# Another hand-written order of work in the stretch between the first feed-forward block and attention

## The reference

```python
x = x + 0.5 * ffn(layernorm(x))      # 8 routed experts
x = x + attn(layernorm(x))           # the stage that matters here
x = x + 0.5 * ffn(layernorm(x))
```

```python
h = (x - mu) * rsqrt(var + eps) * ln_scale + ln_bias     # a second norm, inside attn
c_q, c_kv = h @ w_down_q.T, h @ w_down_kv.T               # latents, 64 wide each
q, k, v = up(c_q), up(c_kv), up(c_kv)                     # 16 heads of 64
q, k = rope(q), rope(k)                                   # rotation by position
out = softmax(q @ k.T / 8) @ v @ w_out.T + residual
```

## Time and profile before

| what | value |
|---|---|
| median of 3 runs | 1592.28 us (1590.46 to 1593.84) |
| profiled execution | 1590.73 us |
| its span on the core | 1588.9 us |
| PE busy | 1520.2 us, 96% |
| DVE busy | 1437.3 us, 90% |
| POOL busy | 1318.8 us, 83% |
| ACT busy | 1254.2 us, 79% |
| chain that ended last | PE 83%, DVE 6%, issue 4%, POOL 3%, ACT 2%, DMA 1% |

### The profile page before, as it was taken

How to read it: one execution, slowest core, us unless ns; L and a number is a source line. 1 busy time by engine, 2 the same in 40 slices (tenths; PEclk the granted TensorE clock), 3 DMA queues, 4 the chain that set the end, 5 groups by cost and what they waited for, 6 DMA issues and landing times.

```text
span 1588.9 us, 48489 instructions
## 1 busy us (share of the span) xinstructions
PE 1520.2 (96%) x19224; PEld 996.8 (63%) x19224; DVE 1437.3 (90%) x2912; ACT 1254.2 (79%) x1764; POOL 1318.8 (83%) x924
## 2 busy tenths in 40 slices
PE   4999869999999999999999999999999999987998
PEld 3777535666666666666666666666666666654555
DVE  6657789999999999999999999999999998967897
ACT  4443577888888888888888888888888888885654
POOL 2566548999999999999999999999999997764666
PEclk9999999999999999999999999999999999999999
DMA  7333130212111121212121211111221212003443
GB/s 203 115 116 118 34 80 12 57 46 53 41 43 42 42 51 43 51 32 52 32 52 45 58 42 42 42 42 46 48 52 32 52 32 52 21 2 101 129 135 120
DMA packets 65727, 95.68 MB, mean 60 GB/s; under 512 B 11744, under 2 KB 24544, under 8 KB 65248
## 3 DMA queue, kind: packets, MB, share of 16 engines
q1 hardware_dynamic: 62416, 91.66, 21.9%
q10 hardware_dynamic: 3088, 0.92, 0.3%
HBM read 39.72 MB, written 2.36 MB: 26 GB/s over the span
## 4 chain that ended last, share of the span: by engine, by line
PE 83%; DVE 6%; issue 4%; POOL 3%; ACT 2%; DMA 1%; ACTq 0%; POOLq 0%; DVEq 0%
PE ps L1020 14%; PE ps L994 14%; PE ps L1021 14%; PE ps L1040 8%; PE ps L1042 8%; PE ps L1038 8%; PE ps L523 3%; PE ps L1009 3%; PE ps L1002 2%; PE ps L501 2%; POOL area L681 2%; PE ps L503 2%; PE ps L502 2%; PE ps L988 2%; PE ps L987 2%
## 5 line engine op out<-in xcount | busy, mean ns | idle before, releaser
L1384 POOL TENSOR_TENSOR area<-area 128x1024 f16<-128x1024 f32 (+1 forms) x512 | 833.5, 1647 | 81.7 <-ACT area L1301 72.6
L1172 DVE TENSOR_REDUCE area<-ps 128x1 f32<-128x512 f32 x1024 | 664.9, 684 | 11.2 <-PE ps L994 8.7
L1299 ACT ACTIVATE area<-ps 128x1024 f16<-128x1024 f32 x512 | 525.5, 1026 | 142.5 <-PE ps L1021 142.3
L1040 PE MATMUL ps<-cv_all,area 128*128 128x64 f16 x4096 | 457.3, 195 | 0.0
L1038 PE MATMUL ps<-cv_all,area 128*128 128x65 f16 x4096 | 455.5, 193 | 0.6 <-POOL area L1384 0.5
L1042 PE MATMUL ps<-cv_all,area 128*128 128x65 f16 x4096 | 454.2, 192 | 0.0
L1040 PEld LDWEIGHTS ps<-cv_all,area 128*128 128x128 f16 x4096 | 381.9, 97 | 78.9 <-issue 0.3
L1038 PEld LDWEIGHTS ps<-cv_all,area 128*128 128x128 f16 x4096 | 384.5, 97 | 60.1 <-issue 9.0
L994 PE MATMUL ps<-area 128*128 128x512 f16 x1024 | 388.5, 380 | 4.8 <-DVE area L1172 4.8
L1020 PE MATMUL ps<-area 128*128 128x512 f16 x1024 | 389.2, 380 | 3.6 <-DVE cv_all L1213 1.1
L1021 PE MATMUL ps<-area 128*128 128x512 f16 x1024 | 389.3, 380 | 0.0
(11 more groups left out here) (173 smaller groups left out, 2265.5 us busy)
## 6 DMA issues: line engine op xcount, KB each, us to landing
area<-area SPq DMA_DIRECT2D x384, 128.0 KB, 2.7
area<-f_w_rows_in_dram SPq DMA_DIRECT2D x126, 256.0 KB, 3.3
xg<-in_x SPq DMA_DIRECT2D x4, 512.0 KB, 9.3
out_x<-xg SPq DMA_DIRECT2D x3, 512.0 KB, 5.0
area<-in_wup SPq DMA_DIRECT2D x1, 1024.0 KB, 9.1
cs<-in_rope SPq DMA_DIRECT2D x1, 1024.0 KB, 9.9
area<-area SPq DMA_DIRECT2D x64, 2.0 KB
area<-in_wg SPq DMA_DIRECT2D x1, 512.0 KB, 7.9
```

The costliest lines, as they stand in the source:

```text
L1040: nc.tensor.matmul(o[:, 0:DH], p_hi[:, s % 4, c:c + P], latents[:, DH + 1:CV], start=False, stop=False, skip_group_check=True)
L1172: nc.vector.tensor_reduce(mx[:, hd, kh, qt:qt + 1], bank, AX.X, ALU.max).then_inc(s_mr, 1)
L1299: nc.scalar.activation(p_hi[:, s % 4, :], sc, ACT.Exp, scale=0.125).then_inc(s_e16, 1)
L1384: nc.gpsimd.tensor_tensor(p_lo[:, s % 4, c0:], src[:, (s // 2) % 2, :], p_hi[:, s % 4, c0:], ALU.subtract).then_inc(s_pp, 1)
```

## The change

Only the four strings change, so the same instructions are issued with the same waits, in another order on each engine.

```diff
-        pe_start = "trrlrrrrtrtrltrrrlrtlataaablaaaaaaaabtalralababmbbbrbSbb"
-        dve_start = "lrrlrrrrrrlNrNrNrNlraaalabaaaaaaaablalraababmbbblrbbb"
-        act_start = "nfnnhfhncxfcfnchfxxcnhfnxhnxxhfxcxfhhc"
-        pool_start = "ssoossssooossooossssoooos"
+        pe_start = "trrtlrrrtrrlrrtlrrtrlaaaatalaaabbtabaaalbalabaabmrrSbbbb"
+        dve_start = "lrrlrrrrrlNrNrNNrlrraaalaaaaabbabalaalbaabaabmlrrbbbb"
+        act_start = "nfnnhfhncfxfnnhchxfccxnhfncfxhxcfxhxxh"
+        pool_start = "ssssoosoosssoooossoossoos"
```

## The result

| | before | changed |
|---|---|---|
| median | 1590.49 us (10 runs, 1587.15 to 1593.84) | 1585.03 us (10 runs, 1582.94 to 1587.35) |
| ratio, 95% interval | | 0.9963 (0.9952 to 0.9973) |
| profiled execution, span | 1590.73, 1588.9 us | 1584.94, 1583.2 us |

The kernel became 5.5 us faster. The 3.7 us between forecast and result are two things: the kernel before measures 1.8 us less here than the 1592.28 that I started from, and the gain is 5.5 us and not 3.6.

What follows compares the result with a forecast made beforehand. TensorE bounds the running units; ahead of unit 0 the limit passes between engines. `S` 4.8 us sooner, less 1.2 for added maxima, makes the mark 3.6 sooner: 1592.28 - 3.6 = 1588.7 us, range 1585.5 to 1591.5.

Steps and rivals of the forecast that it cites:

- Up to the chain: Start through VectorE's norm chain: l2 at 196.36, chain starting 3.08 us sooner and done at 208.64 (before 212.80).
- The stacks' copies: Keys' copies ahead of the first maxima: there at 212.5, their 1.4 us delay hidden because the block is reached at 214.45.
- From l4 to `m`: TensorE's l4 at 210.8, first maxima at 214.45 against 216.75, VectorE's `m` at 234.64 against 237.29, 2.65 us sooner.
- The copied row: Copy of the row of maxima between `m` and scores `S`: taken as 2.1 us, `S` at 237.0 against 241.79.
- the rival of a slow copy: Row copy takes 2.7 to 3.5 us, `S` starts at 237.6 to 238.4: 1589.3 to 1590.1 us; chance 0.17.
- From `S` to the mark: Scores `S` to unit 0's first own score matmul: 4.68 + 1.2 us at half clock, mark at 242.9 against 246.47.
- my first rival: Full clock at `S`: the eight score matmuls run faster, 1.6 us more gained, 1587.1 us; chance 0.20.
- a cost for two more maxima: Between `S` and unit 0, four maxima stand in place of two: 2 x 0.61 = 1.2 us given back.
- the last one, from the stretch to the time: Median 1592.28 less the 3.6 us won at the mark gives 1588.7 us; lists behind the mark taken as unchanged.
- A distance from the mark to the end that differs by over 1 us: Sign of being wrong: the rest of the trace behind the mark was forecast to move by the same amount as the mark.

Runs made afterwards that it cites:

- after_again: Changed kernel once more, no edit, second trace: first rotation to mark (unit 0's first own score matmul) 58.65 us; median 1582.99 us (6 runs).
- after_third: Changed kernel once more, no edit, third trace: first rotation to mark 58.69 us; median 1586.39 us (8 runs).
- combined: Changed kernel with R3.1 ahead of l2, norm chain regrouped around half rotations, and two last maxima ahead of l7: 1585.55 us (ratio 0.9963).
- before_third: Kernel before once more, no edit, third trace: first rotation to mark 63.74 us; median 1589.19 us (12 runs).
- front_only: Changed kernel with the old kind of ending (half of rotation 6 and three maxima ahead of l7): 1588.92 us (ratio 0.9982).
- filled: Changed kernel with TensorE's idle time ahead of l4 filled by repeats of R4.1, R5.0 and t5: 1583.83 us (ratio 0.9950).

## Why the prediction was right and wrong

**Up to the chain: right to 0.1 us.** VectorE has l2 12.60 us behind the first rotation, 3.07 sooner; the third and fourth group, R4.1 and l4 behind R5.1 as worked out (24.72, 26.96). The stacks' copies held nothing up.

**From l4 to `m`: right within 0.5.** Forecast 30.7 and 50.9, measured 30.5 to 31.2 and 50.5 to 51.3. The spread is the clock's.

**The copied row.** I took 2.1 us from the end of `m`. SyncE's queue in the changed kernel:

```profile
233.78 14.58 SPq L1439 DMA_DIRECT2D area<-area  x2
```

`S` began at 235.67 and was released by VectorE, so the row had landed within 1.9 us of its issue. The Trainium skill (DMA: Bandwidth & Descriptors, Anatomy of one DMA) states a fixed cost of about 2.0 us, measured on copies that GpSimd issues; the row here, a copy of SyncE's, shows a little less. `S` came 2.2 us behind the start of `m`, and the sum had 2.4, so the term was about 0.2 too large, or more, and the rival of a slow copy falls.

**From `S` to the mark: right in number at half clock, poor in view.** I took 4.68 + 1.2 = 5.9 at half clock. Two of three traces show 6.0 (after_again, after_third), the first 4.66 with the scores mostly at full clock, as in my first rival. By the means the stretch gave 4.1, not 3.6. The view behind the term was a cost for two more maxima; what counted is that 2.4 us of VectorE's work, not 1.2, lie beside the scores.

**The step that failed is the last one, from the stretch to the time.** I put the forecast on the median of the three runs shown, 1592.28. The kernel before measures 1590.49 over the 10 runs beside the changed kernel and 1589.3 over all 125; three runs of a kernel whose times gather near 1588.8 (65 of 115), 1591.7 (22) and 1593.6 (26) don't fix its median. Put on the profiled execution, as in my own sum, the same 3.6 give 1587.1, and the measured 4.1 give 1586.6. The second half of the same step: I put the change outside the stretch at nothing, on the word of a single trace. The traces show that the start of the first rotation varies from 180.9 to 185.4 and the time behind the mark from 1340.4 to 1343.5, over kernels that have the same instructions there. In the profiled pair, 5.8 us apart, 4.6 lie in the stretch, 1.55 ahead of it, and 0.4 are given back behind it. By the three traces each, 1.4 us of the difference lie ahead of the first rotation (183.74 against 182.33) and 0.6 behind the mark (1342.5 against 1341.9), which with 4.1 makes 6.1, against 5.5 by the means of all runs. A distance from the mark to the end that differs by over 1 us was among my signs of being wrong; after_again and after_third show it.

**What stays open.** Whether those 1.4 and 0.6 us belong to the order. Over the 17 traces the start of the first rotation goes with the clock granted from 20 to 40 us: 180.9 to 182.5 us at 1.00 (6 traces), 182.2 to 183.8 at 0.91 (5), 183.6 to 183.9 at 0.83 (3), 185.2 to 185.4 at 0.74 (3). The time behind the mark goes with the clock from 1400 to 1440 us: 1342.3 to 1343.5 us at 0.91 (14), 1341.4 at 0.96 (2), 1340.4 at 1.00 (1). combined, with the changed kernel's GpSimd and ScalarE strings, started as late (185.4) as the kernel before ever did, so a late start isn't bound to the old order; whether the new order makes it rarer, three traces of each can't tell. The runs at 0.987 and 0.988 don't decide it either: before_third and combined both had 0.74 from 20 to 40 us, but before_third 0.82 and combined 0.90 from 183 to 249 us, and 0.08 of these 66 us is 5.3 us in 1590, the whole gap between their mean clocks of 0.987 and 0.990: it lies in the stretch itself.

## What to carry to other kernels

When several engines feed one another by hand-written orders, find the engine whose work up to a mark is fixed, add up its idle times and ask of each edit which of them it shrinks; a wait removed on another engine, or a piece made earlier, is worth nothing until that sum falls. Put work of that engine beside the long piece it can't help waiting for. And before you forecast a few tenths of a per cent, ask from how many runs the time before comes, and which half-clock stretches its trace happens to hold.

## What the runs showed of the hardware

The lower level of TensorE's clock, half of 2.4 GHz, goes with most of the scatter in the times of this kernel. Busy time of two stretches in three traces, of before_third, after_again and front_only in this order:

```profile
20.00:40.00 20.00, 17.66 (x82) 11.54 (x81) 14.09 (x60) 8.36 (x18) 4.49 (x3) 0.74 0.46 162
1400.00:1440.00 40.00, 31.37 (x463) 22.00 (x462) 21.01 (x69) 32.22 (x52) 20.86 (x14) 0.91 0.07 23
```

```profile
20.00:40.00 20.00, 17.03 (x110) 11.80 (x108) 17.28 (x71) 10.17 (x21) 6.48 (x5) 1.00 0.49 178
1400.00:1440.00 40.00, 28.55 (x392) 19.74 (x389) 21.48 (x58) 29.09 (x53) 19.00 (x13) 0.96 0.14 44
```

```profile
20.00:40.00 20.00, 17.10 (x110) 11.85 (x108) 17.34 (x71) 10.41 (x21) 6.24 (x5) 1.00 0.50 179
1400.00:1440.00 40.00, 28.81 (x438) 19.95 (x435) 22.32 (x62) 31.66 (x55) 19.84 (x13) 1.00 0.13 41
```

With a granted clock of 1.00 in the first stretch the first rotation starts at 180.9 and 181.1 us, with 0.74 at 185.2. With 0.91, 0.96 and 1.00 in the second stretch, the time from mark to end is 1342.5, 1341.4 and 1340.4. So 1 us at half clock costs about 0.4 us in the first stretch (4.2 for 10.2) and 0.3 in the second (1.0 to 1.1 for each step of 0.04 to 0.05 of 40 us, about 3.5 us at half clock), both estimates from these rows. In the changed kernel it holds for 13.6 us, in which TensorE waits 2.0 to 3.7 us at a time for VectorE; in filled, where repeated work with no use stands in those waits, it ends at about 203 us. The Trainium skill (TensorE: Matmul & The Clock Gate, Part 1) says that the throttled state is the default and activity releases it; filled and the changed kernel agree with that: 1.00 in 203 to 212 us against 0.50 in 198.8 to 212.4.
